# The C product of a state, moved between the two scans of the next one

## The chip, the cores and the metric

The kernel runs on one core of a Trainium2 chip. The metric is the device time of one launch in microseconds (us), as the median of several runs. The profile is that of one further execution, taken by the hardware profiler. PE is TensorE, PEld its weight loads, DVE is VectorE, ACT is ScalarE, POOL is GpSimd and SP is SyncE, which issues the DMAs.

## The reference

The model is a stack of sixteen layers on a residual stream of width 128: attentions, mixtures of experts, and in the middle two state-space layers with a dense feed-forward block behind each of them. The change lies in the stage that computes these four. Of the reference this is what matters:

```python
# L2_attn_a, for each of 4 blocks of 256 tokens; L2_attn_b is alike, with two scans (y1 - y2) over one x
delta = softplus(dt_in @ dt_proj_w.T + dt_proj_b)
def step(h, inp):
    d_t, B_t, C_t, u_t = inp
    dA = jnp.exp(d_t[:, :, None] * A)
    h = h * dA + (d_t * u_t)[:, :, None] * B_t[:, None, :]
    y = jnp.einsum('bdn,bn->bd', h, C_t)
    return (h, y)
y = y + x_conv * D
out = einsum('bld,md->blm', y * silu(z), out_proj_w)
# L2_ffn
h = silu(x @ w1.T * s1) * (x @ w2.T * s2)
h = gelu(h @ h1.T * sh1); h = gelu(h @ h2.T * sh2)
out = h @ w3.T * s3
```

There are 256 inner channels and 16 states (n). The recurrence over time is independent for each channel and each state.

## The kernel before, in words

The function `scans_and_dense` computes this stage. Tokens are taken in chunks of 512 columns (CHUNK); the 256 channels are two halves of 128 partitions. A turn is one chunk with one set of scan weights. There are 12 turns (4 of the first state-space layer, 8 of the second, two per chunk), each with 16 states, so 192 steps s = 16 t + n. A step is one state of one turn. The work of a step is:

- ACT computes the decay factors of either half, exp(delta * A), into one of three PSUM banks (`decays`, L2160; the factor with number i = 2s + half waits for scan i-3, whose bank it takes).
- POOL multiplies delta * u by the B row into `s_dbu` (L2418), three steps ahead, in a ring of five.
- DVE scans each half over time (`scan`, L2548, a tensor_tensor_scan from PSUM and `s_dbu` into `s_hh`, a ring of four states). It waits for its decay factor, for `s_dbu` and for the term of state s-4.
- The state is multiplied by its C row. In 60 steps (five of each turn) POOL does it (L2425), with a row spread by a DMA. In the other 132 steps DVE does it (`times_c`, L2556), on both halves at once, from PSUM bank 3: PE spreads the row there by a matmul with 0/1 weights, the pick (`pick_c`, L2034). There is one such bank, so the pick of a state waits for DVE's product of the state before, and the product waits for its pick.
- PE adds the term to the sum y by four transposing matmuls per half (`add_up`, L2052), three steps later.

Beside the steps other work is dealt out by tables. Each step has two slots, 2n and 2n+1. `chain` holds the preparation of later turns (convolution L1889, projections L1857, the split of B and C into bf16 parts L1863 and L1868, the rates with softplus L2212 to L2217 on ACT). `beside` and `dense_slot` hold six of the eight chunks of the dense layers: 51 slots each, with the gate matmuls (L1999), the up matmuls (L2003), two hidden layers (L1977), and the output (L2015). These share one PSUM bank, SPARE: a matmul there waits until ACT or DVE has read the one before. On ACT, L2283 keeps a result, and `bend` (L2287 to L2292) loads a table, applies Silu or Gelu to all four tiles, and loads the first table again. DVE's slots hold the up product (`product`, L2502, which multiplies the up matmul in SPARE by the gate), the gate of y (L2490), additions to the residual (L2495, L2508) and a few single operations such as the taps of the second layer's convolution (L2462).

Every engine runs its own queue in the written order; semaphores do the rest. PE's step is: chain and dense part of slot 2n, `add_up(s - 3, 0)`, chain and dense part of slot 2n+1, `add_up(s - 3, 1)`, `pick_c(s)`. ACT's step is: `decays(s + 1, 0)`, slot 2n, `decays(s + 1, 1)`, slot 2n+1. DVE's step is the loop that the diff edits: both scans of s, slot 2n, the product of s-1, slot 2n+1. The last two chunks of the dense layers follow behind the steps.

Of the kernel before, what the change touches and what calls it, by code (L numbers as in the profile page):

```python
# [1611 lines left out]
def scans_and_dense(g):  # L1612
# [9 lines left out]
    JOBS, TURNS = 2 * CHUNKS, 3 * CHUNKS  # L1622
    STEPS, SLOTS = TURNS * N, 2 * N
# [38 lines left out]
    def by_vector(s):  # L1662
        return s % N not in pool_states(s // N)

    def pool_steps(s):
        return s // N * 5 + sum(n < s % N for n in pool_states(s // N))

    def vector_steps(s):
        return s - pool_steps(s)
# [17 lines left out]
    def ended_job(t):  # L1687

        return job_of(t) - 1 if t and first_turn_of(job_of(t)) == t else None

    def out_slot(t):
        return 17 if t == FIRST else BACK_AT[ended_job(t)] - SLOTS * t + 4
# [32 lines left out]
    with stage(g, InnerNorm.SEMAPHORES + " tables_cast decay_ready negated through_ready minus_ready taps_ready turned_over conv_ready conv_kept z_there z_kept "  # L1725
# [80 lines left out]
        with nc.Block() as block:  # L1806
# [652 lines left out]
            def _(dve):  # L2459
                def make_taps(w):  # L2460
                    taps = w["taps"].rearrange("p (k c) -> p k c", k=TAPS)
                    nc.vector.tensor_tensor(taps, taps, w["in"][:, 0:2 * P].unsqueeze(1).broadcast_to([P, TAPS, 2 * P]),  # L2462
                                            ALU.mult).then_inc(taps_ready, 1)
# [21 lines left out]
                def gate(j, half):  # L2485
                    dve.wait_ge(spare_ready, spare_at[("back", j, half)] + 1)
                    z_there_all(dve, j)
                    if j:
                        dve.wait_ge(pre_ready, pre_at[("out", j - 1)] + 1)
                    nc.vector.tensor_tensor(y[:, half, :], z[:, j % Z_RING, half, :], SPARE, ALU.mult).then_inc(spare_free, 1)  # L2490

                def add(j):
                    dve.wait_ge(pre_ready, pre_at[("out", j)] + 1)
                    x = fixed(g.resid, j % CHUNKS)
                    nc.vector.tensor_tensor(x, x, PRE, ALU.add).then_inc(pre_free, 1)  # L2495

                def product(d, i):
                    m = ORDER[i]
                    dve.wait_ge(spare_ready, spare_at[(d, ("up", m))] + 1)
                    if i:  # L2500
                        dve.wait_ge(gated, 3 * d + i)
                    nc.vector.scalar_tensor_tensor(out=low[:, m, :], in0=SPARE, scalar=ffn["s2"][:, m:m + 1], in1=high[:, m, :],  # L2502
                                                   op0=ALU.mult, op1=ALU.mult).then_inc(spare_free, 1)

                def add_dense(d):
                    dve.wait_ge(spare_ready, spare_at[(d, "out")] + 1)
                    x = fixed(g.resid, d % CHUNKS)
                    nc.vector.scalar_tensor_tensor(out=x, in0=SPARE, scalar=ffn["s3"], in1=x, op0=ALU.mult, op1=ALU.add).then_inc(spare_free, 1)  # L2508

                def slot(t, s):  # L2510

                    at = SLOTS * t + s
                    if at - 1 in back_slot:
                        gate(*back_slot[at - 1])
                    if ended_job(t) is not None and s == out_slot(t) + 2:
                        add(ended_job(t))
                    if at in dense_slot:
                        d, o = dense_slot[at]
                        if o in (15, 17, 19, 21):
                            product(d, (o - 15) // 2)  # L2520
                        if o == 50:
                            add_dense(d)
                    if t == 0 and s == 28:
                        dve.wait_ge(g.loaded["l2b"], 16)
                        make_taps(two)
                        c_columns = two["xall1"].rearrange("p (h c) -> p h c", h=2)[:, :, 48:64]
                        nc.vector.tensor_scalar(c_columns, c_columns, -1.0, None, ALU.mult).then_inc(turned_over, 1)
                    if t == 1 and s == 0:
                        nc.vector.tensor_tensor(skip[:, 0, :], two["d0"], two["d1"], ALU.subtract).then_inc(turned_over, 1)
                        dve.wait_ge(decay_ready, 3)  # L2530
                        nc.vector.tensor_scalar(decay[:, 1:3, :], decay[:, 1:3, :], -1.0, None, ALU.mult).then_inc(negated, 1)
                    if t == 1 and s == 2:
                        dve.wait_ge(turned_over, 2)
                        for half in range(2):
                            nc.vector.tensor_scalar(through[:, 1, half, :], g.ident, skip[:, 0, half:half + 1], None, ALU.mult).then_inc(through_ready, 1)

                def scan(s, half):
                    i = 2 * s + half
                    dve.wait_ge(da_ready, i + 1)
                    if s:  # L2540
                        dve.wait_ge(dbu_ready, s)
                    else:
                        dve.wait_ge(first_made, half + 1)
                    if s >= 4 and by_vector(s - 4):
                        dve.wait_ge(term_vector, vector_steps(s - 4) + 1)
                    elif s >= 4:
                        dve.wait_ge(term_pool, pool_steps(s - 4) + 1)
                    nc.vector.tensor_tensor_scan(hh[:, s % 4, half, :], DECAYS[i % 3], dbu[:, s % D_RING, half, :], 0.0,  # L2548
                                                 ALU.mult, ALU.add).then_inc(scan_done, 1)

                def times_c(s):
                    dve.wait_ge(scan_done, 2 * s + 2)
                    dve.wait_ge(c_spread, vector_steps(s) + 1)
                    if s >= 4:
                        dve.wait_ge(y_added, 2 * (s - 4) + 2)
                    nc.vector.tensor_tensor(term[:, s % 4], hh[:, s % 4], both(PICK_C), ALU.mult).then_inc(term_vector, 1)  # L2556
# [18 lines left out]

                for s in range(STEPS + 1):
                    t, n = divmod(s, N)
                    for half in range(2):
                        if s < STEPS:
                            scan(s, half)  # L2580
                    if t < TURNS:
                        slot(t, 2 * n)
                    if s >= 1 and by_vector(s - 1):
                        times_c(s - 1)
                    if t < TURNS:
                        slot(t, 2 * n + 1)
                gate(JOBS - 1, 0)
                gate(JOBS - 1, 1)
# [1178 lines left out]
```

## Time and profile before

| | |
|---|---|
| median of 3 runs | 3375.11 us (the others 3370.81 and 6977.01) |
| profiled execution | 3378.47 us |
| its span | 3376.8 us |
| mean granted clock of PE | 0.872 |
| PE, DVE, ACT, POOL busy over the span | 88%, 65%, 51%, 31% |

The span runs from the first to the last instruction of the program; some 1.7 us of the execution's own time lie around it. The kernel is a row of stages, one per layer or group of layers, so busy shares of the whole span mix stages with different limits. A row of the timeline or of the waits gives the engine, the line of the kernel, the tile written and the tiles read; the number in brackets is idle time of that engine before the instruction, with the instruction that ended it.

### The profile page before, as it was taken

How to read it: one execution, taken by the hardware profiler on the slowest of the kernel's cores; microseconds unless marked ns; L12 is line 12 of the kernel's file. 1: busy time of each engine (PE TensorE's matmuls, PEld its weight loads, DVE VectorE, ACT ScalarE, POOL GpSimd, SP SyncE). 2: the span in 40 equal slices, each digit the busy share in tenths (PEclk: the TensorE clock that was granted, in tenths of full speed). 3: DMA queues.
4: the chain of work that ended last, by engine and by line, in shares of the span. 5: the costliest groups of instructions: out<-in, count | busy, mean ns of one | idle time of the engine just before them, and what ended most of it. 6: DMA issues, size and time to landing. Idle time of an engine off the chain costs nothing. (4 is left out here: it accounts for less than half of the span.)

```text
span 3376.8 us, 58548 instructions
## 1 busy us (share of the span) xinstructions
PE 2974.8 (88%) x21857; PEld 1713.0 (51%) x21857; DVE 2205.1 (65%) x5852; ACT 1731.0 (51%) x3881; POOL 1051.6 (31%) x464
## 2 busy tenths in 40 slices
PE   7888899998788888889896888887989899989998
PEld 3333344444777777764343444444454344565547
DVE  6777544545666666665648888787782458944991
ACT  3555531523444444442636776676763456744762
POOL 1111100000000000000008879777790207941990
PEclk8999999998555555579997999998999899999999
DMA  5434232031000000003053223222220201240225
GB/s 150 109 89 109 61 125 66 1 109 56 3 3 3 3 3 3 3 2 103 7 167 119 87 75 105 78 90 79 76 82 0 97 1 50 88 187 25 88 88 187
DMA packets 113500, 234.34 MB, mean 69 GB/s; under 512 B 13760, under 2 KB 50752, under 8 KB 104768
## 3 DMA queue, kind: packets, MB, share of 16 engines
q1 hardware_dynamic: 113216, 230.59, 21.4%
q8 instruction: 174, 2.85, 0.3%
q14 instruction: 110, 0.90, 0.1%
HBM read 185.71 MB, written 44.83 MB: 68 GB/s over the span
## 5 line engine op out<-in xcount | busy, mean ns | idle before, releaser
L1249 PE MATMUL psum<-h_ring,h_parts 128*128 128x4 bf16 (+2 forms) x12288 | 418.1, 170 | 121.0 <-ACT h_ring L1337 121.0
L2548 DVE TENSOR_TENSOR_SCAN s_hh<-psum,s_dbu 128x512 f32<-128x512 f32 x384 | 447.2, 1206 | 77.4 <-ACT psum L2160 77.2
L2418 POOL TENSOR_TENSOR s_dbu<-s_du,s_bb 128x1024 f32<-128x1024 f32 x191 | 446.5, 2357 | 64.5 <-DVE s_hh L2548 55.6
L1249 PEld LDWEIGHTS psum<-h_ring,h_parts 128*128 128x128 bf16 x12288 | 372.3, 105 | 171.1 <-ACT h_ring L1337 144.8
L1337 ACT ACTIVATE h_ring<-h_pre 128x16 f32<-128x16 f32 x1024 | 168.3, 211 | 357.5 <-DVE h_pre L1399 357.5
L2160 ACT ACTIVATE psum<-s_delta,s_decay 128x512 f32<-128x512 f32 x384 | 256.5, 686 | 107.3 <-DVE s_hh L2548 105.1
L901 POOL MEMSET r_weights<- 128x512 f32 x4 | 2.1, 524 | 929.8 <-POOLq L1222 660.6
L2052 PEld LDWEIGHTS psum<-w_c,s_term 128*128 128x128 f32 x1536 | 200.8, 150 | 135.2 <-issue 116.3
L910 DVE TENSOR_TENSOR f_hid<-f_gate,psum 128x512 f32<-128x512 f32 x184 | 126.4, 687 | 204.7 <-PE psum L836 197.9
L1399 DVE TENSOR_REDUCE h_pre<-psum 128x16 f32<-128x48 f32 x1024 | 164.7, 202 | 142.2 <-PE psum L1249 142.2
L897 ACT ACTIVATE f_gate<-psum 128x512 f32<-128x512 f32 x184 | 109.6, 597 | 281.6 <-PE psum L832 281.5
L2052 PE MATMUL psum<-w_c,s_term 128*128 128x128 f32 x1536 | 232.2, 288 | 9.0 <-ACT s_y L2238 8.5
L1404 DVE TENSOR_TENSOR h_ring<-h_ring 128x16 f32<-128x16 f32 x1024 | 147.7, 175 | 89.3 <-ACT h_ring L1337 89.3
L2556 DVE TENSOR_TENSOR s_term<-s_hh,psum 128x1024 f32<-128x1024 f32 x132 | 158.9, 1204 | 50.0 <-PE psum L2034 22.9
L475 ACT ACTIVATE a_pt<-psum 128x512 f32<-128x512 f32 (+3 forms) x256 | 108.6, 438 | 137.0 <-PE psum L302 136.3
L3323 POOL TENSOR_TENSOR x_raw<-x_raw,x_mx 128x2048 f32<-128x2048 f32 x32 | 115.9, 3621 | 191.3 <-DVE x_mx L3377 191.3
L2425 POOL TENSOR_TENSOR s_term<-s_hh,s_cc 128x1024 f32<-128x1024 f32 x60 | 141.4, 2357 | 46.1 <-DVE s_hh L2548 24.2
L589 DVE CUSTOM_DVE_ANT_0 a_seen<-psum,c_bf 128x128 bf16<-128x128 f32 (+3 forms) x256 | 115.0, 488 | 61.5 <-PE psum L277 61.1
L1326 ACT ACTIVATE h_lay<-h_xt,w_c 128x32 f32<-128x32 f32 x496 | 152.4, 307 | 0.0
L522 POOL TENSOR_SCALAR_AFFINE_SELECT a_pt<-a_pt 128x512 f32<-128x512 f32 x64 | 42.5, 664 | 352.2 <-ACT a_pt L475 352.2
L1409 DVE TENSOR_TENSOR h_ring<-h_ring 128x16 f32<-128x16 f32 x1024 | 147.4, 175 | 0.0
L3122 PE MATMUL psum<-w_l3f,normed 128*128 128x512 f32 x256 | 130.8, 591 | 0.0
(533 smaller groups left out, 6259.9 us busy)
## 6 DMA issues: line engine op xcount, KB each, us to landing
s_bb<-s_wide SPq DMA_DIRECT2D x192, 256.0 KB, 3.4
x_spill<-x_flip SPq DMA_DIRECT2D x28, 1024.0 KB, 3.8
f_share<-f_wide SPq DMA_DIRECT2D x208, 128.0 KB, 3.0
s_cc<-s_wide SPq DMA_DIRECT2D x60, 256.0 KB, 3.3
a_ks<-a_spread SPq DMA_DIRECT2D x96, 128.0 KB, 3.3
a_qs<-a_spread SPq DMA_DIRECT2D x96, 128.0 KB, 3.9
x_spare<-x_spill SPq DMA_DIRECT2D x4, 2048.0 KB, 7.6
x_raw<-x_spill SPq DMA_DIRECT2D x4, 2048.0 KB, 7.7
```

Source lines behind the costliest of these rows:

```text
L1249: mm = nc.tensor.matmul(columns_of(s // BLOCK, grp)[:, s % BLOCK, 0:3 - part, cols], parts[:, part, GROUP * grp + p, :], upper[:, (s - 1) ...
L1326: done = nc.scalar.activation(lay[:, blk % 2, grp, :, col:col + BATCH], xt[:, blk * BLOCK:(blk + 1) * BLOCK, :], ACT.Identity, scale=g.pai ...
L1337: nc.scalar.activation(ring[:, (n - 1) % TURN, grp, 0, :], pre[:, grp, :], ACT.Tanh).then_inc(state[grp], 1)
L1399: nc.vector.tensor_reduce(pre[:, grp, :], columns_of(s // BLOCK, grp)[:, s % BLOCK, :, :].rearrange("p q c -> p c q"), AX.X, ALU.add).then ...
L1404: nc.vector.tensor_tensor(ring[:, s, grp, 1, :], ring[:, s, grp, 0, :], upper[:, s, grp, 0, :], ALU.subtract).then_inc(rest[grp], 1)
L1409: nc.vector.tensor_tensor(ring[:, s, grp, 2, :], ring[:, s, grp, 1, :], upper[:, s, grp, 1, :], ALU.subtract).then_inc(last[grp], 1)
L2052: mm = nc.tensor.matmul(turned(q, half), term[:, s % 4, half, q * P:(q + 1) * P], g.ident, is_transpose=True, start=(fresh and half == 0 a ...
L2160: nc.scalar.activation(DECAYS[i % 3], delta[:, t % 2, half, :], ACT.Exp, scale=decay[:, a, half * N + n:half * N + n + 1]).then_inc(da_rea ...
L2418: nc.gpsimd.tensor_tensor(dbu[:, s % D_RING], du[:, t % 2], both(bb[:, s % B_RING, :]), ALU.mult).then_inc(dbu_ready, 1)
L2425: nc.gpsimd.tensor_tensor(term[:, s % 4], hh[:, s % 4], both(cc[:, pool_steps(s) % C_RING, :]), ALU.mult).then_inc(term_pool, 1)
L2548: nc.vector.tensor_tensor_scan(hh[:, s % 4, half, :], DECAYS[i % 3], dbu[:, s % D_RING, half, :], 0.0, ALU.mult, ALU.add).then_inc(scan_do ...
L2556: nc.vector.tensor_tensor(term[:, s % 4], hh[:, s % 4], both(PICK_C), ALU.mult).then_inc(term_vector, 1)
```

## The change

The loop over the steps on DVE is written in another order. Within a step the first scan of state s comes first, then the C product of state s-1 (if DVE has it), then slot 2n, then the second scan of state s, then slot 2n+1. No other engine's queue changes, and no instruction is added or taken away.

```diff
                 for s in range(STEPS + 1):
                     t, n = divmod(s, N)
-                    for half in range(2):
-                        if s < STEPS:
-                            scan(s, half)
-                    if t < TURNS:
-                        slot(t, 2 * n)
+                    if s < STEPS:
+                        scan(s, 0)
                     if s >= 1 and by_vector(s - 1):
                         times_c(s - 1)
                     if t < TURNS:
+                        slot(t, 2 * n)
+                        scan(s, 1)
                         slot(t, 2 * n + 1)
```

On DVE, at the end of the first turn, before the change (L2548 is a scan, which the listing names by its operand form, L2556 the C product, L2462 and L2527 the taps and columns of the second layer):

```order
L2548 SCALAR_TENSOR_TENSOR s_hh<-psum,s_dbu 128x512 x4
L2556 TENSOR_TENSOR s_term<-s_hh,psum 128x1024
L2548 SCALAR_TENSOR_TENSOR s_hh<-psum,s_dbu 128x512 x2
L2462 TENSOR_TENSOR w_l2b<-w_l2b 128x1024
L2527 TENSOR_SCALAR w_l2b<-w_l2b 128x2x16
L2556 TENSOR_TENSOR s_term<-s_hh,psum 128x1024
L2548 SCALAR_TENSOR_TENSOR s_hh<-psum,s_dbu 128x512 x2
```

The same place after the change:

```order
L2548 SCALAR_TENSOR_TENSOR s_hh<-psum,s_dbu 128x512 x4
L2556 TENSOR_TENSOR s_term<-s_hh,psum 128x1024
L2548 SCALAR_TENSOR_TENSOR s_hh<-psum,s_dbu 128x512 x2
L2556 TENSOR_TENSOR s_term<-s_hh,psum 128x1024
L2462 TENSOR_TENSOR w_l2b<-w_l2b 128x1024
L2527 TENSOR_SCALAR w_l2b<-w_l2b 128x2x16
L2548 SCALAR_TENSOR_TENSOR s_hh<-psum,s_dbu 128x512 x2
```

The taps now stand behind a C product and ahead of the second scan of their step.

On DVE, the up products of the second dense chunk (L2502; L2495 adds to the residual, L2556 and L2548 as above), before:

```order
L2548 SCALAR_TENSOR_TENSOR s_hh<-psum,s_dbu 128x512 x2
L2502 SCALAR_TENSOR_TENSOR s_low<-psum,w_l2f,s_high 128x512
L2556 TENSOR_TENSOR s_term<-s_hh,psum 128x1024
L2548 SCALAR_TENSOR_TENSOR s_hh<-psum,s_dbu 128x512 x2
L2502 SCALAR_TENSOR_TENSOR s_low<-psum,w_l2f,s_high 128x512
L2556 TENSOR_TENSOR s_term<-s_hh,psum 128x1024
```

and after:

```order
L2548 SCALAR_TENSOR_TENSOR s_hh<-psum,s_dbu 128x512 x2
L2556 TENSOR_TENSOR s_term<-s_hh,psum 128x1024
L2502 SCALAR_TENSOR_TENSOR s_low<-psum,w_l2f,s_high 128x512
L2548 SCALAR_TENSOR_TENSOR s_hh<-psum,s_dbu 128x512 x2
L2556 TENSOR_TENSOR s_term<-s_hh,psum 128x1024
L2502 SCALAR_TENSOR_TENSOR s_low<-psum,w_l2f,s_high 128x512
```

Each up product of this chunk was ahead of the C product and behind both scans; now it is behind the C product and ahead of the second scan.

## Rows read from the trace of the kernel before

**Rows 1.** The page: busy time (share of the span) xinstructions.

```profile
PE 2974.8 (88%) x21857; PEld 1713.0 (51%) x21857; DVE 2205.1 (65%) x5852; ACT 1731.0 (51%) x3881; POOL 1051.6 (31%) x464
```

**Rows 2.** Windows: the stage; length, busy us and instructions per engine, clock, DMA.

```profile
1774.00:2548.00 774.00, 649.40 (x2585) 365.50 (x2584) 630.57 (x573) 532.62 (x764) 621.69 (x272) 0.92 0.28 86
```

**Rows 3.** Waits of DVE in the stage: us in total, times, longest us.

```profile
DVE s_hh L2548 <- ACT psum L2160: 77.2, 45, 7.0
DVE s_term L2556 <- PE psum L2034: 22.9, 12, 5.6
DVE s_term L2556 <- issue: 22.5, 15, 3.4
...
DVE s_term L2556 <- DVE s_hh L2548: 4.3, 10, 0.7
```

**Rows 4.** Waits of PE in the stage.

```profile
PE psum L2034 <- DVE s_term L2556: 39.7, 24, 9.4
PE psum L2003 <- DVE s_low L2502: 14.0, 8, 3.5
PE psum L2003 <- ACT s_high L2289: 12.7, 5, 5.6
```

**Rows 5.** Waits of ACT in the stage.

```profile
ACT psum L2160 <- DVE s_hh L2548: 105.1, 109, 6.8
ACT s_high L2283 <- PE psum L1977: 35.0, 16, 4.4
ACT s_low L2283 <- PE psum L1977: 23.4, 13, 4.1
```

**Rows 6.** Groups of instructions in the stage, by form: busy us, mean ns | idle before.

```profile
L2548 DVE TENSOR_TENSOR_SCAN s_hh<-psum,s_dbu 128x512 f32<-128x512 f32 x384 | 447.2, 1206 | 77.4 <-ACT psum L2160 77.2
L2556 DVE TENSOR_TENSOR s_term<-s_hh,psum 128x1024 f32<-128x1024 f32 x132 | 158.9, 1204 | 50.0 <-PE psum L2034 22.9 <-issue 22.5 <-DVE s_hh L2548 4.3
```

**Rows 7.** Timeline of DVE and PE: three stretches with a late second scan.

```profile
1799.13 1.22 DVE L2548 TENSOR_TENSOR_SCAN s_hh<-psum,s_dbu 128x512 f32<-128x512 f32 x1 [1.68 <-ACT psum L2160]
...
2011.45 1.22 DVE L2548 TENSOR_TENSOR_SCAN s_hh<-psum,s_dbu 128x512 f32<-128x512 f32 x1 [3.10 <-ACT psum L2160]
2012.59 0.72 DVE L2502 SCALAR_TENSOR_TENSOR s_low<-psum,w_l2f,s_high 128x512 f32<-128x512 f32 x1
2013.37 1.89 PE L2003 MATMUL psum<-normed,w_l2f 128*128 128x512 f32 x2 [3.24 <-DVE s_low L2502]
2014.36 2.33 DVE L2548 TENSOR_TENSOR_SCAN s_hh<-psum,s_dbu 128x512 f32<-128x512 f32 x2
...
2506.89 1.22 DVE L2548 TENSOR_TENSOR_SCAN s_hh<-psum,s_dbu 128x512 f32<-128x512 f32 x1 [3.33 <-ACT psum L2160]
```

**Rows 8.** The window with full PE, and a late pick in it on the timeline.

```profile
2376.00:2390.00 14.00, 14.00 (x48) 7.03 (x47) 7.51 (x7) 4.42 (x7) 11.50 (x5) 1.00 0.21 56
...
2387.93 0.38 PE L2034 MATMUL psum<-s_bc,c_bf 96*128 96x512 bf16 x1
2388.41 1.22 DVE L2556 TENSOR_TENSOR s_term<-s_hh,psum 128x1024 f32<-128x1024 f32 x1 [4.21 <-PE psum L2034]
```

**Rows 9.** Timeline of DVE and PE around the taps.

```profile
1826.71 1.22 DVE L2548 TENSOR_TENSOR_SCAN s_hh<-psum,s_dbu 128x512 f32<-128x512 f32 x1 [1.61 <-ACT psum L2160]
1827.85 5.57 DVE L2462 TENSOR_TENSOR w_l2b<-w_l2b 128x1024 f32<-128x1024 f32 x1
1834.69 0.61 PE L2034 MATMUL psum<-s_bc,c_bf 96*128 96x512 bf16 x1 [9.39 <-DVE s_term L2556]
```

**Rows 10.** Late up products: the window behind one, then two places on the timeline.

```profile
2013.00:2017.00 4.00, 3.63 (x8) 1.84 (x9) 4.00 (x5) 2.20 (x4) 0.00 (x0) 0.57 0.00 0
...
2237.14 1.22 DVE L2548 TENSOR_TENSOR_SCAN s_hh<-psum,s_dbu 128x512 f32<-128x512 f32 x1 [2.31 <-ACT psum L2160]
2239.06 1.22 PE L2003 MATMUL psum<-normed,w_l2f 128*128 128x512 f32 x1 [3.46 <-DVE s_low L2502]
...
2471.61 1.22 DVE L2548 TENSOR_TENSOR_SCAN s_hh<-psum,s_dbu 128x512 f32<-128x512 f32 x1 [0.71 <-ACT psum L2160]
2473.53 0.70 PE L2003 MATMUL psum<-normed,w_l2f 128*128 128x512 f32 x1 [3.46 <-DVE s_low L2502]
```

## The prediction

> **What bounds the kernel now.** The page comes first. PE is busy for 88% of the span and DVE for 65% [rows 1], but these are averages over stages with different limits, so the stage that the diff edits is read alone. Its scans start at 1773.9 us and its last C product at 2546.5 us. In that stretch of 774 us [rows 2] PE is busy for 649.4 us, DVE for 630.6, POOL for 621.7 and ACT for 532.6. No engine is full: PE, the busiest, idles for 125 us and DVE for 143 us. The stage is bound by how four queues, each with a fixed order, meet.
>
> Next, who waits for whom there. DVE [rows 3] waits for ACT's decay factors before a scan (77.2 us, 45 times), and before its C product for the pick matmul of PE (22.9 + 22.5 + 4.3 = 49.7 us under three names, 37 waits). The names "issue" and "s_hh" are the pick too: the scan that the product reads is then long over, and the pattern is that of rows 8, where the pick (L2034) starts 0.48 us before the product. PE [rows 4] waits for DVE's C product before the next pick (39.7 us, 24 times, the longest 9.4), for the up product (14.0), and for ACT's bent gate before an up matmul (12.7). ACT [rows 5] waits for scans (105.1) and for dense matmuls (35.0 + 23.4 = 58.4 for the hidden layers). Neither list has POOL among its larger entries, so POOL has slack.
>
> These waits form loops. ACT bends a hidden layer or softens a rate, with table loads of 1.28 us around it; the next decay is late; DVE stands; the C product behind the scan is late; PE stands at the pick. Where PE is densest the loop runs the other way: from 2376 to 2390 us PE is busy 14.00 of 14.00 us and DVE 7.51 [rows 8].
>
> **The change, part by part.** It removes and adds no instruction: 384 scans of 1206 ns and 132 products of 1204 ns stay [rows 6]. Back to back they overlap a little: two scans take 2.33 us together [rows 7] where one takes 1.21 [rows 6], so one more scan or product in front of another costs 1.12 us. Two things move. In each of the 132 steps with a DVE product, the product of state s-1 passes the second scan of state s. And the first slot of the step (gate, up product, the slow taps) passes that scan too, now behind the C product instead of ahead of it.
>
> First term, the late pick. PE's 24 waits for the product total 39.7 us; without the longest they are 30.3 us in 23, or 1.3 us each. All of them end at least 1.12 us sooner when the product need not let the second scan by, and more when that scan is itself standing for its decay. In the trace this is common: of the 45 decay waits, 30 stand before the second scan of a state, and 26 of these have a C product in the step, the first at 1799.13 us (1.68 us long), the last at 2506.89 (3.33) [rows 7]. There the product needs nothing that is missing and would run inside the wait. I count 1.12 us for the waits that are that long and the whole of the shorter ones: some 22 us of PE's time. The ceiling is the whole 39.7.
>
> The longest wait is a case of its own. At 1827.85 the taps of the second layer take 5.57 us in a first slot, ahead of the product, and PE waits 9.39 us [rows 9]. Now the product runs at about 1825, as the second scan waits. But the next product still has the taps ahead of it. Counting DVE's pieces, only the scan's wait (1.61) comes off; it is inside the 22 above.
>
> Second term, the up products. PE waits three times some 3.3 us for an up product, where it stands in a first slot behind a second scan that lacks its decay. In rows 7 the second scan waits 3.10 us to 2011.45, the product starts at 2012.59, and PE resumes at 2013.37 after 3.24 us. With the slot ahead of that scan the product starts at about 2009.5, and PE loses nothing. The other two (waits of PE to 2239.06 and 2473.53, 3.46 each; the scans' waits before them 2.31 and 0.71) shrink by 1.12 plus the scan's wait: 3.4 and 1.8. Together 3.2 + 3.4 + 1.8 = 8.4 us [rows 7, 10].
>
> Third term, what is given back. The product that passes the scan also meets its own wait sooner. The 37 waits for a pick begin 1.12 us earlier, with a scan now queued behind them, and behind that scan ACT's next decay (three PSUM banks: factor i waits for scan i-3) and POOL's next inputs. At worst 37 x 1.12 = 41 us of DVE idle come on top; at best none of it counts, since PE is full in those places and DVE catches up. Which it is, the trace of before cannot show. Against it: a decay has more room towards PE's side. From the end of product s-2, which releases PE for step s, to the first scan that needs ACT's slot of that step, the old order leaves two steps, the new one two steps and one operation. The same room is taken from the way ACT to PE to pick. Of the 41 us I take a quarter, 10, nearer the lower end, since rows 8 show PE without a gap. The 12 up products of the odd slots (layers 0, 2, 4; half of the 24) stay at the end of the step but are now one scan further behind the C product that lets PE go: 0 to 12 x 1.12 = 13 us, of which I take 3, since PE's waits for up products other than the three above sum to only 14.0 - 10.2 = 3.8 us [rows 4, 10].
>
> The sum is 22 + 8.4 - 10 - 3 = 17 us. The profiled execution took 3378.5 us (span 3376.8), so its like would be 3361; the median of the runs is 3.4 us lower, at 3375.1, and from it the forecast is 3358 us. The bounds of the terms are -(39.7 + 8.4) and +(41 + 13 - 22 - 8.4), or 48 us less to 24 us more.
>
> PE's clock is a term of its own. Behind PE's wait of 3.24 us to 2013.37 [rows 7] the granted clock of the four us from 2013 is 0.57, most of them at the half level (1.2 of 2.4 GHz) [rows 10]. Over the stage the clock is 0.92 [rows 2]. If fewer idle stretches follow, some of those 8% come back: half of them, on 649 us of work, is 26 us. I leave this out of the sum, since the many pauses that ACT alone makes remain.
>
> The Trainium skill, "TensorE: Matmul & The Clock Gate", Part 1, says that the array's clock is gated to half while PE is idle and returns to full after sustained work. The trace agrees (0.57 behind the pause). By that rule the saving would be larger than the waits it removes, which is the first rival below.
>
> **The rivals.** *The clock comes back too.* If the 30 us of removed waits also remove most of the slow stretches, the gain is 17 + 26 = 43 us, or 3332; with the give-back at nothing and all of PE's 39.7 us gone, 3375 - 48 - 26 = 3301. For it: the fall of the clock right behind a wait for an up product. Against it: PE's waits for ACT's bent gate [rows 4] (12.7 us) do not hang on DVE's order directly, and they too stop PE, for up to 5.6 us at a time.
>
> *Slower: the second scan behind the late pick.* The mechanism is the 37 pick waits. It decides if the decay of the second scan is already there when the product stands waiting, and ACT's next factor then comes too late for the scan of the next step, so that PE's next pick is late as well. At 41 us against 30 it gives +11; with the odd up products +24: 3386 to 3399. For it: DVE waits for picks (49.7 us) longer than PE waits for products (39.7). Against it: PE is full there, and a full PE decides the step.
>
> *Nothing.* The ring of three decay factors and the alternation scan, scan, product repeat as before; only the meeting with PE shifts. If room gained on one side is lost on the other, the time is 3370 to 3380.
>
> **How the numbers follow.** Forecast of a small gain (3340 to 3368): 0.45. Nothing (3368 to 3382): 0.22. Clock too (below 3340): 0.17, of which 0.05 beyond 2%. Slower: 0.16, of which 0.02 beyond 2%. The range 3325 to 3392 takes in the bounds of the sum (3375 - 48 to 3375 + 24 = 3399) but for their ends, and a part of the clock's gain. Two per cent is 67.5 us, about what a measurement of this kernel can tell from no change, so nearly all of this lies within it: faster 0.05, same 0.93, slower 0.02.
>
> **What would show it.** In the changed profile the waits of PE for the C product should fall from 39.7 to below 20 us, those for the up product from 14.0 to about 9; DVE's waits before the product should grow from 49.7 to 60 or more, and its decay waits shrink. The stage should take some 757 us instead of 774. If the decay waits do not shrink, or PE's waits for ACT grow by as much as those for DVE fall, the third term was too small. If the granted clock of the stage rises above 0.94, the first rival is at work.

## The result, and the profile after

The changed kernel takes 3389.6 us (median of 5 runs, 3385.3 to 3393.4), the kernel before 3377.4 in the same comparison. The ratio is 1.0042, with a 95% interval of 1.0025 to 1.0059. That is slower by some 14 us, where the forecast was faster by 17. One run of the kernel before took 6977 us and is left out of the ratio. The time lies inside the stated range, but the sign is wrong.

The profiled execution has a span of 3385.1 us. The page's busy times are those of [rows 1] to within 5 us per engine:

```profile
PE 2970.7 (88%) x21857; PEld 1709.7 (51%) x21857; DVE 2204.1 (65%) x5852; ACT 1732.6 (51%) x3881; POOL 1052.9 (31%) x464
```

The stage runs from the first scan to the end of the last C product: from 1771.3 to 2558.6 us, or 787.4 us, against 773.8 before. The window over it answers to [rows 2]: length, busy us and instructions per engine, clock, DMA.

```profile
1771.00:2559.00 788.00, 649.49 (x2587) 364.13 (x2587) 628.15 (x574) 535.29 (x765) 622.45 (x272) 0.93 0.27 85
```

PE is busy for 649.5 us as before, and its granted clock is 0.93 against 0.92. So all of the loss is idle time of PE: 788 - 649.5 = 138.5 us against 124.6. The waits say where it arose. First those of PE in the changed kernel's stage (us in total, times, longest), which answer to [rows 4]:

```profile
PE psum L2034 <- DVE s_term L2556: 20.4, 14, 5.2
PE psum L2003 <- ACT s_high L2289: 15.1, 6, 5.6
PE psum L2052 <- ACT s_y L2238: 10.4, 5, 4.1
PE psum L1863 <- ACT s_bc L2196: 10.2, 5, 4.2
PE psum L2003 <- DVE s_low L2502: 10.1, 7, 3.1
PE psum L1999 <- ACT s_high L2283: 6.7, 6, 2.4
```

Of those that [rows 4] does not show, the kernel before has:

```profile
PE psum L2052 <- ACT s_y L2238: 8.5, 5, 4.1
PE psum L1863 <- ACT s_bc L2196: 8.2, 3, 4.2
...
PE psum L1999 <- ACT s_high L2283: 3.2, 3, 1.7
```

The wait for the C product fell from 39.7 to 20.4 us, or by 19, near the 22 of the first term. It was replaced by many small waits, most of them for ACT. Then DVE and ACT, which answer to [rows 3] and [rows 5]:

```profile
DVE s_term L2556 <- PE psum L2034: 52.6, 13, 6.9
DVE s_term L2556 <- issue: 48.0, 22, 3.6
DVE s_hh L2548 <- ACT psum L2160: 36.7, 21, 4.4
...
DVE s_term L2556 <- DVE s_hh L2548: 9.5, 20, 0.8
```

```profile
ACT psum L2160 <- DVE s_hh L2548: 167.3, 142, 5.7
ACT s_high L2283 <- PE psum L1977: 21.9, 11, 4.4
ACT s_low L2283 <- PE psum L1977: 17.0, 11, 4.1
```

DVE's waits for decay factors are halved (77.2 to 36.7 us), but its waits for the pick are more than doubled: 52.6 + 48.0 + 9.5 = 110.1 us against 49.7. ACT waits 167.3 us for scans, against 105.1.

Two places show how. The first is the prediction's own example of a step with nothing to lose, the second scan that waits 1.68 us to 1799.13 [rows 7]. In the kernel before, the pick that the product needs stands here (start, length, engine, line, idle time before it):

```profile
1798.75 0.38 PE L2034 MATMUL psum<-s_bc,c_bf 96*128 96x512 bf16 x1
```

The scan's wait began at 1797.45, so a product put into it would have stood 1.3 us for a pick that had not started. In the changed kernel it does stand, 1.73 us long, and the second scan, whose factor is now there, stands behind it:

```profile
1797.27 0.63 PE L2034 MATMUL psum<-s_bc,c_bf 96*128 96x512 bf16 x1
...
1798.00 1.22 DVE L2556 TENSOR_TENSOR s_term<-s_hh,psum 128x1024 f32<-128x1024 f32 x1 [1.73 <-PE psum L2034]
1799.14 1.22 DVE L2548 TENSOR_TENSOR_SCAN s_hh<-psum,s_dbu 128x512 f32<-128x512 f32 x1
```

So it is in most of the 26 steps that the prediction counted so. In 16 of them the pick of the kernel before starts later than the scan's wait, by 0.2 to 5.9 us. In the changed kernel 15 of the 26 products wait, for 50.3 us together against 14.7, while the wait of the second scans there falls from 43.6 to 9.4 us. The two together are 58 us before and 60 after: at these steps DVE's waiting changed its name and not its length.

The second place shows how such a wait reaches PE over ACT. It is the gate phase of the last of the six dense chunks. First the timeline of the kernel before:

```profile
2457.87 1.22 DVE L2556 TENSOR_TENSOR s_term<-s_hh,psum 128x1024 f32<-128x1024 f32 x1 [1.59 <-issue]
...
2459.11 0.69 ACT L2283 ACTIVATE s_high<-psum,w_l2f 128x512 f32<-128x512 f32 x1
...
2460.01 1.02 PE L1999 MATMUL psum<-normed,w_l2f 128*128 128x512 f32 x2
```

The C product waits 1.59 us for its pick, and nothing is hurt: both scans of the state were done, so ACT's factors do not stand, its slot follows at 2459.11, and PE goes on at 2460.01 without a pause. The same place in the changed kernel:

```profile
2467.01 1.22 DVE L2556 TENSOR_TENSOR s_term<-s_hh,psum 128x1024 f32<-128x1024 f32 x1 [2.12 <-issue]
...
2468.15 1.22 DVE L2548 TENSOR_TENSOR_SCAN s_hh<-psum,s_dbu 128x512 f32<-128x512 f32 x1
...
2469.40 0.69 ACT L2160 ACTIVATE psum<-s_delta,s_decay 128x512 f32<-128x512 f32 x1 [1.66 <-DVE s_hh L2548]
...
2470.03 0.67 ACT L2283 ACTIVATE s_high<-psum,w_l2f 128x512 f32<-128x512 f32 x1
...
2470.75 1.12 PE L1999 MATMUL psum<-normed,w_l2f 128*128 128x512 f32 x2 [1.31 <-ACT s_high L2283]
```

The product waits 2.12 us with the second scan behind it. The scan ends at 2469.37; ACT's next factor has stood 1.66 us for it; the read of SPARE is queued behind that factor, and PE, which needs SPARE, stands for 1.31 us. The lateness of PE's pick has come back to PE over DVE and ACT.

### The profile page after: what moved, and what is told of

The parts are those of the page before. It is cut to its first block and busy times, and to the rows that moved or that the text cites. A ratio compares the mean times of both kernels' runs of the same rounds, so it can differ in the third digit from the quotient of the medians.

```text
span 3385.1 us, 58548 instructions
## 1 busy us (share of the span) xinstructions
PE 2970.7 (88%) x21857; PEld 1709.7 (51%) x21857; DVE 2204.1 (65%) x5852; ACT 1732.6 (51%) x3881; POOL 1052.9 (31%) x464
## 3 DMA queue, kind: packets, MB, share of 16 engines
q1 hardware_dynamic: 113216, 230.59, 21.2%
## 5 line engine op out<-in xcount | busy, mean ns | idle before, releaser
L2548 DVE TENSOR_TENSOR_SCAN s_hh<-psum,s_dbu 128x512 f32<-128x512 f32 x384 | 446.2, 1206 | 37.8 <-ACT psum L2160 36.7
L2160 ACT ACTIVATE psum<-s_delta,s_decay 128x512 f32<-128x512 f32 x384 | 258.1, 687 | 169.5 <-DVE s_hh L2548 167.3
L2556 DVE TENSOR_TENSOR s_term<-s_hh,psum 128x1024 f32<-128x1024 f32 x132 | 159.3, 1207 | 110.4 <-PE psum L2034 52.6
L2425 POOL TENSOR_TENSOR s_term<-s_hh,s_cc 128x1024 f32<-128x1024 f32 x60 | 141.4, 2356 | 56.4 <-DVE s_hh L2548 54.7
```

The source lines that it names most:

```text
L2160: nc.scalar.activation(DECAYS[i % 3], delta[:, t % 2, half, :], ACT.Exp, scale=decay[:, a, half * N + n:half * N + n + 1]).then_inc(da_rea ...
L2425: nc.gpsimd.tensor_tensor(term[:, s % 4], hh[:, s % 4], both(cc[:, pool_steps(s) % C_RING, :]), ALU.mult).then_inc(term_pool, 1)
```

## The experiments

Ten kernels were run. The theories that the expectations name are these. Theory 1: a product that passes the second scan holds it up, and with it what waits for that scan; by 1a the loss comes back to PE over DVE's slots behind the scan, by 1b over ACT's next factor and the slots queued behind that. Theory 2: the loss is in the place of slot 2n. Theory 3: ACT's slots are late for their own length.

The table has for each kernel the length of the stage in its profiled execution, PE's busy time and granted clock there, and the idle time, in us: PE in total and by what ended it (only waits over 0.1 us; "slots" are the results of DVE's slots, L2490 to L2508), DVE before its scans and before its C product, ACT for scans. Profiled spans of the rest of the program differ by up to 15 us between these runs, so the stage is the sharper measure of where time goes, and the ratio to the kernel before that of whether it counts.

| kernel | stage | PE busy | clock | PE idle | PE for product | PE for ACT | PE for slots | scan for factor | product for pick | ACT for scan |
|---|---|---|---|---|---|---|---|---|---|---|
| before | 773.8 | 649.3 | 0.918 | 124.1 | 40.5 | 55.0 | 21.2 | 77.4 | 49.8 | 105.8 |
| changed | 787.4 | 648.9 | 0.928 | 138.2 | 21.2 | 76.0 | 29.2 | 37.7 | 110.4 | 167.7 |
| product alone | 813.3 | 659.4 | 0.918 | 153.8 | 21.9 | 72.8 | 48.6 | 39.5 | 133.8 | 174.2 |
| slot alone | 770.5 | 645.0 | 0.927 | 125.2 | 47.7 | 54.4 | 12.5 | 69.6 | 39.8 | 126.8 |
| all slots ahead | 790.9 | 645.8 | 0.935 | 145.0 | 25.9 | 85.4 | 21.5 | 32.0 | 109.0 | 170.6 |
| changed, ACT early | 784.9 | 650.8 | 0.922 | 133.5 | 32.8 | 52.1 | 40.1 | 88.2 | 62.5 | 99.5 |
| before, ACT early | 800.6 | 660.9 | 0.906 | 139.6 | 60.4 | 38.4 | 32.2 | 136.8 | 26.4 | 68.3 |
| changed, four places | 808.3 | 665.3 | 0.907 | 142.6 | 26.9 | 53.3 | 35.3 | 18.7 | 73.0 | 120.9 |
| before, four places | 806.6 | 660.0 | 0.911 | 146.6 | 45.3 | 48.4 | 36.4 | 55.8 | 37.3 | 74.3 |
| 26 late picks | 784.1 | 651.5 | 0.922 | 132.4 | 44.8 | 62.3 | 15.5 | 59.4 | 70.0 | 140.9 |
| 20 late factors | 762.5 | 643.6 | 0.932 | 118.8 | 40.3 | 53.3 | 15.1 | 40.3 | 63.3 | 120.8 |
| nine steps | 762.8 | 641.5 | 0.933 | 121.3 | 43.5 | 54.7 | 13.4 | 59.1 | 42.3 | 115.7 |

Two cautions go with it. Each row is one execution. The rest of the program, which is the same in all, scatters by 15 us in 2600; the same share of the stage would be 4 to 5 us (an estimate), so smaller differences in the first column say little. And PE's busy time is not the same in all rows, though its instructions are. For the most part it is low where the granted clock of the stage is high (641.5 us at 0.933) and high where the clock is low (665.3 us at 0.907). A difference in length is thus waits and clock together.

**The two moves apart.** The change moves the product and the slot. Either was made alone; both edits are shown against the changed kernel.

```diff
-                        slot(t, 2 * n)
-                        scan(s, 1)
+                        scan(s, 1)
+                        slot(t, 2 * n)
                         slot(t, 2 * n + 1)
```

> Order on DVE: first scan, C product of s-1, second scan, slot 2n, slot 2n+1: the product is moved alone, the slot stays behind both scans. Theory 1 (the product takes the second scan's place, so ACT's next decay factor and the dense slots queued behind it on ACT come later relative to PE, and PE waits for ACT): the stage takes as long as in the changed kernel or a little more, 785 to 793 us (before 774), PE's waits for ACT stay near 76 us (before 55). Theory 2 (the loss comes from the slot's place: DVE stands in slot 2n for a matmul with the second scan behind it): the stage falls back to about 774 us.

```diff
-                    if s < STEPS:
-                        scan(s, 0)
-                    if s >= 1 and by_vector(s - 1):
-                        times_c(s - 1)
                     if t < TURNS:
+                        scan(s, 0)
                         slot(t, 2 * n)
                         scan(s, 1)
+                    if s >= 1 and by_vector(s - 1):
+                        times_c(s - 1)
+                    if t < TURNS:
                         slot(t, 2 * n + 1)
```

> Order on DVE: first scan, slot 2n, second scan, C product of s-1, slot 2n+1: the slot is moved alone. Theory 1: nothing is lost; PE's three long waits for up products (3.2 + 3.5 + 3.5 us) shrink and the stage takes 764 to 774 us, with PE's waits for ACT at about 55. Theory 2: the stage takes 780 us or more, as in the changed kernel.

With the product moved alone the median is 3412.5 us against 3375.1, a ratio of 1.0121 (1.0097 to 1.0144); the stage takes 813.3 us, far above the 793 that was expected at most. With the slot moved alone it is 3369.2 us, a ratio of 0.9986 (0.9975 to 0.9996); the stage takes 770.5 us. Theory 2 falls: the slot's place is the good half of the change. The product costs 37 us alone, and the slot's move takes 23 of them back (26 in the stage). It does so mainly through the results of DVE's slots, for which PE waits 48.6 us with the product moved alone, and 29.2 with both. PE's waits in the run with the product moved alone:

```profile
PE psum L2034 <- DVE s_term L2556: 21.3, 15, 8.5
PE psum L2003 <- DVE s_low L2502: 18.0, 8, 3.5
...
PE psum L1977 <- DVE s_low L2502: 7.3, 5, 2.7
PE psum L1988 <- DVE resid L2508: 7.0, 4, 3.6
```

and with the slot moved alone, where the wait for the up product is halved from the 14.0 of [rows 4]:

```profile
PE psum L2034 <- DVE s_term L2556: 41.9, 26, 8.4
...
PE psum L2003 <- DVE s_low L2502: 7.0, 7, 1.5
```

What the slot gives alone is small: 6 us of time. In the stage it is 3 us, and PE's idle time there did not fall (125.2 us against 124.1): it waits 9 us less for slots and 7 us more for products; the stage is shorter by PE's busy time, at a higher clock. The kernel with the product moved alone has 10 us more of PE's busy time than the kernel before (660.0 us in its window against 649.4), at the same granted clock of 0.918. The surplus is spread over many lines, none with more than 2.4 us, and its cause is open.

**All slots ahead of the second scan.** Is the loss in the slots that remain behind that scan, or in the scan?

```diff
                         slot(t, 2 * n)
-                        scan(s, 1)
                         slot(t, 2 * n + 1)
+                        scan(s, 1)
```

> The changed kernel with slot 2n+1 ahead of the second scan too: first scan, C product, slot 2n, slot 2n+1, second scan. In the run with the product moved alone PE waited 49 us for results of DVE's slots (up product, residual, gate of y), in the changed kernel 29, in the kernel before 21. Theory 1a (a slot behind the second scan is late by that scan relative to the product that lets PE go, and that is the larger part of the loss): with no slot behind it these waits fall to 20 us or less and the stage from 787 to 772 to 780 us. Rival 1b (the loss is the second scan itself, which holds up ACT's factors and the slots behind them on ACT): these waits move by less than 5 us or others take their place, and the stage stays at 783 to 792 us.

PE's waits for slots fell from 29.2 to 21.5 us, and its waits for ACT rose from 76.0 to 85.4. The stage takes 790.9 us and the ratio is 1.0051 (1.0032 to 1.0070). Rival 1b holds: the larger part is the second scan, and what ACT has queued behind it.

**ACT's slots ahead of its factors.** If ACT's slots are late because a factor in front of them waits for a scan, they may pass that factor.

```diff
-                    if s + 1 < STEPS and s + 1 > 2:
-                        decays(s + 1, 0)
                     slot(t, 2 * n)
                     if s + 1 < STEPS and s + 1 > 2:
-                        decays(s + 1, 1)
+                        decays(s + 1, 0)
                     slot(t, 2 * n + 1)
+                    if s + 1 < STEPS and s + 1 > 2:
+                        decays(s + 1, 1)
```

> The changed kernel with ACT's slot 2n ahead of its first decay factor of a step and slot 2n+1 ahead of the second, so that a dense or chain operation no longer stands behind a factor that waits for a late scan. Theory 1: PE's waits for ACT fall from 76 to 60 us or less and the stage from 788 to 764 to 778 us. Theory 3 (ACT's slots are late for their own lengths, table loads above all, and not for the factor ahead of them): PE's waits for ACT stay within 5 us of 76 and the stage within 4 us of 788, or longer since the factors now come later.

> The kernel before with the same two swaps on ACT. Theory 1: there the slots' way to PE had more room already and the way from PE over ACT to the scans was the short one, so the swap gives less than in the changed kernel: the stage takes 770 to 785 us (before 774), with DVE's waits for decay factors above their 77 us. Theory 3: the same change as in the run on the changed kernel, in sign and size.

In the changed kernel PE's waits for ACT fell from 76.0 to 52.1 us, so the factor in front was the cause of that part and theory 3 falls. But the stage fell only from 787.4 to 784.9 us (ratio to before 1.0031, 1.0018 to 1.0045), outside what theory 1 gave: the factors now come later, scans wait 88.2 us for them, and PE waits for products (32.8) and slots (40.1) instead. In the kernel before the same swap costs 27 us of stage (ratio 1.0101, 1.0083 to 1.0120), more than expected; scans wait 136.8 us for their factors. That the swap costs one order much and the other nothing that can be measured (the intervals of the changed kernel with and without it overlap) fits theory 1: the old order has no room to spare on the way from ACT to the scans, the new one has.

**Four places for the factors.** The other cure is a ring in which factor i waits for scan i-4. PSUM has no bank left, so the fourth place is in SBUF.

```diff
-    DECAYS = (bank[1], bank[4], bank[5])
+        DECAYS = (bank[1], bank[4], bank[5], sb("s_fourth", [P, CHUNK])[:, :])
...
-                    if i >= 3:
-                        act.wait_ge(scan_done, i - 2)
+                    if i >= 4:
+                        act.wait_ge(scan_done, i - 3)
```

Where a factor is written and where it is read, `i % 3` becomes `i % 4`.

> The changed kernel with four places for decay factors instead of three (the fourth in SBUF), so that factor i waits for scan i-4. Theory 1b (ACT's factor behind a late scan is what makes PE wait for ACT): ACT's waits for scans fall from 167 to below 100 us, PE's waits for ACT from 76 to 60 or less, the stage from 787 to 770 to 779 us, and most of the difference to the kernel before with four places is gone. Theory 1a (DVE's late slots): the stage stays within 5 us of 787 and the difference to the kernel before with four places stays 10 us or more.

> The kernel before with four places for decay factors. Theory 1b: ACT waited 105 us for scans here too, so it gains, but less than the changed kernel: the stage takes 762 to 774 us (before 773.8), DVE's waits for factors fall from 77 us. Theory 1a: 765 to 775 us too; the two runs tell the theories apart only together.

Both kernels became slower, by ratios of 1.0094 (1.0069 to 1.0118) and 1.0107 (1.0087 to 1.0127), against every expectation. A scan that reads its factor from SBUF takes longer there, as the last section shows. How that made the stage longer was not shown: in the changed order PE's idle time rose by only 4 us (138.2 to 142.6) and its busy time by 16, at a clock of 0.907 against 0.928. As a cure this says nothing. But the difference between the two orders is gone: 808.3 and 806.6 us of stage, 3408.6 and 3413.1 us of time. In the changed order ACT's waits for scans fell to 120.9 us, where 1b gave below 100, and PE's waits for ACT to 53.3. That fits 1b, though with longer scans in both it is weaker evidence than the runs above.

**Chosen steps.** The last three runs start from the slot-alone order and let the product pass the second scan in some steps only. The edit is that of the run with nine steps, against the changed kernel; the other two differ in the list.

```diff
+                    early = s in (14, 30, 60, 72, 88, 110, 142, 159, 180)
                     if s < STEPS:
                         scan(s, 0)
-                    if s >= 1 and by_vector(s - 1):
+                    if early and by_vector(s - 1):
                         times_c(s - 1)
                     if t < TURNS:
                         slot(t, 2 * n)
                         scan(s, 1)
+                    if s >= 1 and by_vector(s - 1) and not early:
+                        times_c(s - 1)
+                    if t < TURNS:
                         slot(t, 2 * n + 1)
```

> Slot 2n ahead of the second scan in every step; the C product passes the second scan only in the 20 steps in which the trace of the kernel before shows that scan waiting for its decay factor (6, 14, 30, 46, 52, 59, 60, 66, 72, 86, 88, 93, 98, 110, 125, 130, 142, 157, 159, 180). Theory 1 (the move pays where the scan waits for ACT and costs where the product waits for PE): the stage takes 755 to 768 us, below the 770.5 of the run with the slot moved alone, with PE's waits for the product below 35 us (47.7 there). Rival (the steps that wait depend on the order and shift when it changes, so a choice by the old trace gives nothing): 768 to 778 us.

> Slot 2n ahead of the second scan in every step; the C product passes that scan in 26 steps in which the trace of the kernel before shows DVE waiting for the pick, and in which the scan has its factor in time. Theory 1 (the move costs where the product waits for PE, since the second scan then stands behind that wait): slower than the 770.5 us of the run with the slot moved alone, stage 777 to 795 us, with DVE's waits for picks up by 15 us or more from their 40, and PE's waits for ACT above 60. Rival (the loss comes from moving all 132 products together, which gives every queue another phase, and not from single steps): within 5 us of 770.5.

> As the run with 20 chosen steps, but the product passes the second scan in nine of them (14, 30, 60, 72, 88, 110, 142, 159, 180): in most of the others that run's trace shows the product itself waiting 1.8 to 4.7 us for its pick, with the scan behind it. Theory 1: these nine carry the gain, so the stage takes 758 to 767 us and the median 3360 to 3368. Rival (both sides of the 20 matter, or a choice this fine is lost in the scatter between executions): 768 us or more for the stage, or a median that the run with the slot alone (3369) can't be told from.

Where the scan was waiting longest for its factor (20 of the 26 steps, all waits of 1.0 us and more among them), the stage takes 762.5 us, 8 less than with the slot alone; the median moved by only 1 us, to 3368.1 (ratio 0.9982, 0.9970 to 0.9994), so this gain is seen in the stage alone. PE's waits for the product fell to 40.3 us, not below the expected 35. Where the product was waiting for its pick (26 steps), it takes 784.1 us, 14 more than with the slot alone (half of it idle time of PE and half busy time), at 3380.7 us (ratio 1.0020, 1.0011 to 1.0030). DVE's waits in that run, against 39.8 us for picks with the slot alone:

```profile
DVE s_hh L2548 <- ACT psum L2160: 58.1, 31, 6.8
DVE s_term L2556 <- issue: 47.5, 23, 3.8
DVE s_term L2556 <- PE psum L2034: 20.7, 8, 5.7
```

So single steps carry the loss, as theory 1 says: the interval of this run lies clear of that with the slot alone. The nine steps give 762.8 us of stage and the best median, 3364.8 us against 3374.2, a ratio of 0.9975 (0.9965 to 0.9984). This version is faster than both kernels, if by a quarter of a per cent. Its interval overlaps those of the run with 20 steps and of the slot alone (0.9975 to 0.9996), so that chosen steps add to the slot's gain rests on the two profiled stages alone (762.5 and 762.8 us against 770.5). Against the kernel before, 8 of the 11 us of the nine steps' stage are PE's busy time (641.5 us against 649.3, at a clock of 0.933 against 0.918), and 3 are waits.

What the nine steps have in common stands in the trace of the kernel before: in seven the pick starts before the scan's wait does, and in the other two (60 and 180) at most 1.0 us behind. In the 11 that were left out it starts 1.3 to 5.0 us behind.

## Why the prediction was wrong, point by point

- **That the loss or gain would lie in PE's idle time, in this stage:** right. PE's busy time is 649.5 us in both, and the stage is longer by its idle time.
- **First term, 22 us of PE's waits for the C product:** right in size. 39.7 fell to 20.4, and DVE's waits for factors from 77.2 to 36.7. Its reason was wrong: "There the product needs nothing that is missing and would run inside the wait." In 16 of those 26 steps the pick had not started when the scan's wait began. The trace of before shows it, and so did the late pick of [rows 8]: it belongs to one of the 26.
- **Second term, 8.4 us at three up products:** right in place and size. The three waits of 3.24, 3.46 and 3.46 us became 1.59, 0 and 0.39, a saving of 8.2. That the whole row fell only from 14.0 to 10.1 is due to other waits, above all a new one where the up product now stands behind the C product:

```profile
2018.33 0.70 PE L2003 MATMUL psum<-normed,w_l2f 128*128 128x512 f32 x1 [1.59 <-DVE s_low L2502]
...
2481.85 0.70 PE L2003 MATMUL psum<-normed,w_l2f 128*128 128x512 f32 x1 [0.39 <-DVE s_low L2502]
...
2487.17 0.70 PE L2003 MATMUL psum<-normed,w_l2f 128*128 128x512 f32 x1 [3.10 <-DVE s_low L2502]
```

- **Third term, what is given back:** here it failed. "Of the 41 us I take a quarter, 10, nearer the lower end, since rows 8 show PE without a gap." DVE's waits for picks rose not by at most 41 us but by 60 (49.7 to 110.1). The 37 products that had waited account for 32 of it, and 21 others that now met an unfinished pick for 29; by place, 36 of the 60 lie in the 26 steps of the first term. And a full PE at the moment of the wait says nothing of the steps behind it: PE's waits for ACT rose by 21 us and for DVE's slots by 8. Together with smaller ones they outweigh the 19 us saved at the product. The term was bounded by counting the waits that existed, which is no bound for a wait that the change can create.
- **The 3 us for the odd up products:** the two that stand behind the second scan and wait longer for it cost 1.6 us more together (0.84 to 1.30 and 0.27 to 1.38). What the sum had no term for are the other slots: PE waits 6 us more for additions to the residual and 3 us more for the gate of y.
- **The rival "slower"** had the right place and, in part by luck, the right price (+11 to +24 us; measured in the stage +13.6), with a chance of 0.16. Its path back to PE was another one: late factors for the next step's scan, and by them late picks. Those did not come, for DVE's waits for factors halved and so did PE's for products. The loss came through what is queued behind the factor on ACT, and through DVE's slots.
- **The clock** was left out of the sum, and in the changed kernel it gave nothing back: 0.918 became 0.928, below the 0.94 that was named as a sign, with PE's busy time as before. In the runs that removed waits (20 and nine steps) it rose to 0.93 and PE's busy time fell by 6 and 8 us. That is what the first rival describes, at a quarter to a third of its 26 us.
- **Two per cent, 67.5 us, as what a measurement can tell from no change** was far too wide. Here 14 us stood clear, with an interval of some 6 us to either side.

## What to carry to other kernels

When two queues wait for each other, moving an item forward in one shortens the way in one direction and lengthens it in the other; price both with the queue of the third engine that hangs on the item passed. Here the product could pass the scan for nothing where the scan was itself waiting and the product's own pick had already been made; the first alone was not enough. Both can be read from the trace before the change, so list for each step what the moved item needs and when it came. A wait is harmless while nothing that others need stands behind it, so look at what a move puts behind an existing wait, and expect new waits as well as longer ones. A move made of two parts should be timed in parts: one half of this one cost 37 us alone and the other gave 6 us.

## What was not expected of the hardware

A scan with its decay factor in SBUF took 1954 ns on average, against 1200 for one with it in PSUM, in the same run of the changed order with four places (group rows: busy us, mean ns | idle before):

```profile
L2418 POOL TENSOR_TENSOR s_dbu<-s_du,s_bb 128x1024 f32<-128x1024 f32 x191 | 485.7, 2560 | 66.4 <-DVE s_hh L2548 56.2 <-DMA s_bb<-s_wide 9.8
L2548 DVE TENSOR_TENSOR_SCAN s_hh<-psum,s_dbu 128x512 f32<-128x512 f32 x288 | 337.7, 1200 | 15.3 <-ACT psum L2160 12.4 <-POOL s_dbu L2418 2.7
...
L2548 DVE TENSOR_TENSOR_SCAN s_hh<-s_fourth,s_dbu 128x512 f32<-128x512 f32 x96 | 187.6, 1954 | 3.6 <-ACT s_fourth L2160 3.5
```

POOL's multiplications took 2560 ns there instead of 2357. The timeline shows how the two meet:

```profile
1802.34 2.35 POOL L2425 TENSOR_TENSOR s_term<-s_hh,s_cc 128x1024 f32<-128x1024 f32 x1
1803.87 1.90 DVE L2548 TENSOR_TENSOR_SCAN s_hh<-s_fourth,s_dbu 128x512 f32<-128x512 f32 x1
1804.65 3.27 POOL L2418 TENSOR_TENSOR s_dbu<-s_du,s_bb 128x1024 f32<-128x1024 f32 x1
```

The scan starts 0.82 us before POOL's operation ends (1804.69) and ends 1.08 us after it; POOL's next one, which meets the scan, takes 0.9 us longer than its usual 2.36. Of the 96 scans of this kind the shortest took 1.19 us. It looks as if either engine stood for the other's whole instruction. The Trainium skill, "SBUF — State Buffer", section "SBUF: two separate sides", says that a DVE instruction with two SBUF inputs and a GpSimd instruction that reads SBUF lock a shared port pair against each other; the trace agrees. A decay factor in PSUM is thus worth 0.75 us a scan here.
